# Cross-attention and experts in one kernel: key copies ahead of sums on ScalarE, sums dealt otherwise over the bodies, another order of steps among the experts

## What is computed

```python
def xattn(hs, at, mask):                       # 16 heads of 16
    q, k, v = proj(hs, Wq, bq), proj(at, Wk, bk), proj(at, Wv, bv)
    scores = clip(einsum('bhsd,bhtd->bhst', q, k) / 4, -50, 50)
    scores = clip(where(mask > 0.5, scores, -10000.0), -50, 50)
    probs = softmax(scores)
    probs = probs / (probs.sum(-1) + 1e-8)
    ctx = einsum('bhst,bhtd->bhsd', probs, v)
    delta = clip(rs, 0, 0.3) * nan_clean(ctx @ Wo.T + bo)
    return layernorm(delta) * ln_gamma + ln_beta

def ffn(hs):                                   # 8 experts, top 2 by softmax of hs @ router.T
    ...
    h = up * silu(gate)                        # each row in its two experts
    return sum over its two of (h @ down[e]) * score

x = x + tanh(g_xattn) * xattn(layernorm(x), ctx_2048, mask)
x = x + tanh(g_ffn) * ffn(layernorm(x))
```

## Time and profile before

| | |
|---|---|
| median of three runs | 290.21 us (290.14 to 292.1) |
| the profiled execution | 291.79 us, its span 290.1 us |
| TensorE busy | 236.3 us, 81% |
| VectorE busy | 179.2 us, 62% |
| ScalarE busy | 137.8 us, 48% |
| POOL busy | 62.5 us, 22% |
| chain that ended last | TensorE 56%, issue 19%, ScalarE 11%, VectorE 7%, POOL 5% |
| moved by DMA | 37.55 MB |

### The profile page before, as it was taken

The page is one execution under the profiler, slowest core; times in us unless marked ns, Lnnn a source line. Parts: engine busy times, 40 slices in busy tenths (PEclk is TensorE's granted clock), DMA queues, the critical chain, the costliest instruction groups (busy, mean ns, idle before and its releaser), DMA issues.

```text
span 290.1 us, 7184 instructions
## 1 busy us (share of the span) xinstructions
PE 236.3 (81%) x2704; PEld 181.2 (62%) x2704; DVE 179.2 (62%) x415; ACT 137.8 (48%) x220; POOL 62.5 (22%) x102
## 2 busy tenths in 40 slices
PE   0619389999999999859998629399899567999994
PEld 0309268888888888638886529296575336565653
DVE  7677805458899963365298923446379991494535
ACT  5135723567688678854378870220523406620110
POOL 2820021124245111101033200000625246210000
PEclk9999959999999999985999976859999997999998
DMA  7325801296798999988523000030000000020002
GB/s 177 90 54 162 353 5 39 67 329 239 274 292 325 341 385 427 398 260 316 214 83 137 2 0 2 3 64 5 0 0 0 0 0 2 0 63 1 2 0 64
DMA packets 12871, 37.55 MB, mean 129 GB/s; under 512 B 2321, under 2 KB 10017, under 8 KB 10529
## 3 DMA queue, kind: packets, MB, share of 16 engines
q1 hardware_dynamic: 12016, 36.65, 36.8%
q10 hardware_dynamic: 720, 0.40, 0.6%
q0 software_dynamic: 96, 0.00, 0.0%
HBM read 35.14 MB, written 0.92 MB: 124 GB/s over the span
## 4 chain that ended last, share of the span: by engine, by line
PE 56%; issue 19%; ACT 11%; DVE 7%; POOL 5%; DVEq 1%; POOLq 0%; ACTq 0%
PE bank L484 11%; PE bank L491 9%; PE bank L689 8%; PE bank L501 8%; PE bank L512 6%; PE bank L706 5%; ACT ctx_all L802 5%; ACT p L790 4%; POOL x_sb L461 4%; PE bank L476 3%; PE bank L593 1%; PE bank L469 1%; ACT normed L806 1%; PE bank L583 1%; DVE p L1171 1%
## 5 line engine op out<-in xcount | busy, mean ns | idle before, releaser
L790 ACT ACTIVATE p<-bank,mask_bias,mask_scale 125x896 f32<-125x896 f32 x38 | 39.6, 1093 | 43.8 <-PE bank L501 43.8
L484 PE MATMUL bank<-ctx_pair,wk 128*128 128x250 f32 x152 | 40.4, 410 | 5.9 <-issue 5.9
L689 PE MATMUL bank<-rowsT,gate_up 128*128 128x448 f32 x112 | 44.6, 541 | 0.0
L388 POOL COPY q_slot<-qbd 128x224 f32 x38 | 17.1, 453 | 95.2 <-PE bank L501 67.0
L491 PE MATMUL bank<-wv,ctx_pair 128*125 128x256 f32 x152 | 36.9, 387 | 0.0
L1002 DVE TENSOR_SCALAR p<-p 125x912 f32<-125x912 f32 x38 | 28.1, 754 | 14.1 <-ACT p L790 14.1
L484 PEld LDWEIGHTS bank<-ctx_pair,wk 128*128 128x128 f32 x152 | 29.1, 202 | 12.1 <-issue 7.0
L706 PE MATMUL bank<-down,act 128*112 128x256 f32 x128 | 31.8, 393 | 4.5 <-DVE act L1260 3.6
L802 ACT ACTIVATE ctx_all<-ctx_all 128x1500 f32<-128x1500 f32 x24 | 35.1, 1467 | 0.0
L491 PEld LDWEIGHTS bank<-wv,ctx_pair 128*125 128x125 f32 x152 | 29.3, 193 | 4.6
L706 PEld LDWEIGHTS bank<-down,act 128*112 128x112 f32 x128 | 23.1, 184 | 13.8 <-DVE act L1260 4.7
(11 more groups left out here) (147 smaller groups left out, 295.2 us busy)
## 6 DMA issues: line engine op xcount, KB each, us to landing
ctx_all<-ctx_dram SPq DMA_DIRECT2D x16, 1500.0 KB, 6.8
ctx_pair<-ctx_dram SPq DMA_DIRECT2D x38, 125.0 KB, 5.0
gate_up<-gate_up_dram SPq DMA_DIRECT2D x1, 2048.0 KB, 10.0
down<-down_dram SPq DMA_DIRECT2D x1, 1024.0 KB, 11.9
num<-acc SPq DMA_DIRECT2D x16, 57.0 KB, 2.7
x_sb<-x_dram SPq DMA_DIRECT2D x2, 448.0 KB, 6.4
out_dram<-x_sb SPq DMA_DIRECT2D x4, 224.0 KB, 2.4
wq<-wq_dram ACTq DMA_DIRECT2D x1, 256.0 KB, 4.4
```

Source lines behind the costliest of these rows:

```text
L388: nc.gpsimd.tensor_copy(targets[t], source).then_inc(flow.q_in, 1)
L484: mm = nc.tensor.matmul(bank[:, K_BANK, 2 * TT * m:2 * TT * (m + 1)], wk[:, k, P * m:P * (m + 1)], tile[:, :, k, :], start=(k == 0), stop= ...
L689: mm = nc.tensor.matmul(bank[:, GU_BANK[s % 2] + g, 0:HR], gate_up[:, e, k, g, :], rowsT[:, k, HR * h:HR * (h + 1)], start=(k == 0), stop= ...
L790: nc.scalar.activation(p_tile[:, t].rearrange("t (j n) s -> t j n s", j=4)[:, :, :, 0:S], bank[0:TT, 0:4, DEN * t:DEN * (t + 1)].rearrange ...
```

## The change

ScalarE's key copy of body i + 1 now stands behind the exponentials of body i, ahead of the sums. The sums follow two tables: `SUM_BODY[b]` is the body of batch b's first half, `LATER_BODY[b]` that of its second half where ScalarE does it; VectorE now does the second half of ten batches (`SHARE`), ScalarE of six. Bodies 20 and 21 have no sums. SyncE's `fetch_all(b)` stands at i = `SUM_BODY[b]` + 1, before the weights and before `pack(0)`. `add_delta(0, 1)` moves into body 21, `masked_sums(1)` behind pair 21, and among the experts the steps of TensorE, ScalarE, VectorE and POOL stand in another order; `delta_of` is parted in two.

```diff
--- before.py
+++ after.py
@@ -194,6 +194,10 @@
                 "spread1", "spread1b", "out1_0", "out1_1", "hT1_0", "hT1_1", "route1"]
         USE = {name: n for n, name in enumerate(USES)}
 
+        SUM_BODY = [6, 7, 8, 9, 10, 11, 12, 12, 13, 14, 14, 15, 16, 17, 18, 19]
+        LATER_BODY = [6, 7, 8, 9, 10, 11, 12, 13, 14, 15, 15, 16, 17, 18, 19, 19]
+        SHARE = 10
+
         def p_of(h):
             return (h % 8) // 2 * 4 + h // 8 * 2 + h % 2
 
@@ -210,7 +214,10 @@
 
             if b >= 0:
                 engine.wait_ge(sum_first, b + 1)
-                engine.wait_ge(sum_second[b // HB], b % HB + 1)
+                if b < SHARE:
+                    engine.wait_ge(sum_second[0], b + 1)
+                else:
+                    engine.wait_ge(sum_second[1], b - SHARE + 1)
 
         def misc(lo, hi, rows=P):
             return bank[0:rows, MISC_BANK, lo:hi]
@@ -304,15 +311,14 @@
                 sp.dma_start(tile[:], source.partition_broadcast(R2)).then_inc(late_in, 16)
             for i in range(10, NTAIL):
                 fetch_pair(i)
+                for b in range(B):
+                    if b >= STREAMS and SUM_BODY[b] + 1 == i:
+                        fetch_all(b)
                 if i == 16:
                     for tile, source in ((router, router_d), (gate_up, gate_up_d), (down, down_d)):
                         sp.dma_start(tile[:], source).then_inc(experts_in, 16)
                 if i == 19:
                     pack(0)
-                if i - 7 < B:
-                    fetch_all(i - 7)
-            for b in range(NTAIL - 7, B):
-                fetch_all(b)
             pack(1)
             out_rows = out_d.rearrange("(r p) h -> p r h", p=R2)
             for h in range(2):
@@ -445,13 +451,13 @@
             h_guess(1)
 
             for u in range(2 * NE):
-                if u == 4:
+                if u == 6:
                     delta_guess(2)
-                if u == 6:
+                if u == 7:
                     h_guess(2)
-                if u == 8:
+                if u == 10:
                     delta_guess(3)
-                if u == 10:
+                if u == 12:
                     h_guess(3)
                 pool.wait_ge(d_scaled, u + 1)
                 if u < 2:
@@ -707,7 +713,6 @@
                                               act[:, s % 2, R2 * t:R2 * (t + 1)], down[:, e, :], start=True, stop=True)
                     mm.then_inc(d_mm, 1)
 
-            masked_sums(1)
             pair_pv(NTAIL - 2)
             pe.wait_ge(experts_in, 48)
             pe.wait_ge(misc_out, USE["hT0_0"] + 1)
@@ -715,34 +720,37 @@
             expert_half(0, 0)
             expert_half(1, 0)
             pair_pv(NTAIL - 1)
+            masked_sums(1)
             h_transposes(0, 1)
             route(0)
             expert_half(0, 1).then_inc(gu_mm, 1)
             expert_half(1, 1).then_inc(gu_mm, 1)
             pe.wait_ge(main.acc_out, 2 * NTAIL)
             expert_out(0)
+            expert_in(2)
             use("spread1")
             spread_inverse(1, 0, misc(0, 2 * DEN)).then_inc(misc_mm, 1)
-            expert_in(2)
+            expert_out(1)
             use("spread1b")
             spread_inverse(1, 1, misc(0, 2 * DEN)).then_inc(misc_mm, 1)
-            expert_out(1)
             expert_in(3)
             project_out(1, 0)
             expert_out(2)
+            expert_in(4)
             project_out(1, 1)
-            expert_in(4)
             expert_out(3)
             expert_in(5)
             expert_out(4)
+            h_transposes(1, 0)
             expert_in(6)
-            h_transposes(1, 0)
             expert_out(5)
             expert_in(7)
+            expert_out(6)
             h_transposes(1, 1)
-            expert_out(6)
+            expert_out(7)
             route(1)
-            for s in range(NE - 1, 2 * NE):
+            expert_in(8)
+            for s in range(NE, 2 * NE):
                 if s + 1 < 2 * NE:
                     expert_in(s + 1)
                 expert_out(s)
@@ -801,6 +809,13 @@
                 mine = ctx_all[b % STREAMS][:, :, k, :]
                 nc.scalar.activation(mine, mine, ACT.Identity, accum_out=total[:, k, b:b + 1]).then_inc(
                     sum_first if k == 0 else sum_second[1], 1)
+
+            def sums_of(i):
+                for b in range(B):
+                    if SUM_BODY[b] == i:
+                        sum_all(b, 0)
+                    if b >= SHARE and LATER_BODY[b] == i:
+                        sum_all(b, 1)
 
             def normalise_rows(t, done):
                 nc.scalar.activation(normed[:, t], x_sb[:, t], ACT.Identity, bias=offset[:, t:t + 1],
@@ -867,13 +882,14 @@
             act_e.wait_ge(counted, 1)
             tiles = count_of(act_e)
             early_exps(NOPT - 1)
+            k_copy(main, k_sb, NOPT + 1)
             for i in range(NOPT, NTAIL):
-                pair_exps(i)
+                exps(main, p[i % 2], slots_of(i), i + 1)
                 if i == 21:
                     misc_rows(0, 0)
-                sum_all(i - NOPT, 0)
-                if i >= FIRST_B:
-                    sum_all(i - NOPT, 1)
+                if i + 1 < NTAIL:
+                    k_copy(main, k_sb, i + 2)
+                sums_of(i)
                 if i == 20:
                     h_rows(0)
             h_rows(1)
@@ -902,16 +918,19 @@
             gate_silu(1)
             for s in range(NE):
                 scale_expert(s)
-                gate_silu(s + 2)
+                if s == 4:
+                    misc_rows(1, 0)
+                if s == 6:
+                    misc_rows(1, 1)
+                if s == 7:
+                    exps_of_logits(1)
+                    gate_silu(NE)
+                if s != 6:
+                    gate_silu(s + 2)
                 if s == 3:
                     h_rows(2)
-                if s == 4:
-                    misc_rows(1, 0)
+                if s == 5:
                     h_rows(3)
-                if s == 5:
-                    misc_rows(1, 1)
-                if s == 6:
-                    exps_of_logits(1)
             for s in range(NE + 2, 2 * NE):
                 gate_silu(s)
 
@@ -1078,6 +1097,10 @@
                 nc.vector.tensor_tensor(flat, flat, bank[:, V_BANK, 0:2 * DEN], ALU.mult).then_inc(wide_out, 1)
 
             def delta_of(h, n):
+                delta_parts(h, n)
+                delta_whole()
+
+            def delta_parts(h, n):
 
                 dve.wait_ge(misc_mm, USE[f"out{h}_{n}"] + 1)
                 raw = fix_raw[:].rearrange("p n h -> p (n h)")
@@ -1090,7 +1113,12 @@
                 nc.vector.tensor_scalar(fix_neg[0:R2], raw, 0.0, lim[:, 1:2], ALU.min, ALU.max).then_inc(chain, 1)
                 nc.vector.tensor_scalar(finite[0:R2], raw, 0.0, 0.0, ALU.mult, ALU.is_equal).then_inc(chain, 1)
                 count[0] += 3
-                dve.wait_ge(chain, count[0] - 1)
+
+            def delta_whole():
+
+                raw = fix_raw[:].rearrange("p n h -> p (n h)")
+                out = delta[:].rearrange("p n h -> p (n h)")
+                dve.wait_ge(chain, count[0])
                 step(nc.vector.tensor_tensor(out, out, fix_neg[0:R2], ALU.add))
                 nc.vector.tensor_copy(spare[:, 0:1], spare[:, 1:2])
                 step(nc.vector.copy_predicated(out, finite[0:R2], raw))
@@ -1247,9 +1275,12 @@
                 elif i == 20:
                     delta_of(0, 1)
                     clips(main, p[i % 2], 2 * i + 1)
+                elif i == 21:
+                    add_delta(0, 1)
+                    clips(main, p[i % 2], 2 * i + 1)
                 else:
                     clips(main, p[i % 2], 2 * i + 1)
-                if i < FIRST_B:
+                if i - NOPT < SHARE:
                     sum_all(i - NOPT)
                 if i == 15:
                     masked_sums(0)
@@ -1271,31 +1302,32 @@
                                                    ALU.add).then_inc(d_out, 1)
 
             pair_sums(NTAIL - 2)
-            add_delta(0, 1)
+            h_offsets(0, 1)
             pair_sums(NTAIL - 1)
             masked_sums(1)
-            h_offsets(0, 1)
             shift_logits(0)
+            expert_ranks(0)
+            expert_weights(0)
+            gate(0)
             inverses(1)
-            gate(0)
+            gate(1)
             totals(1)
             misc_mix(0, "spread1")
-            gate(1)
-            expert_ranks(0)
-            expert_weights(0)
+            gate(2)
             misc_mix(1, "spread1b")
-            gate(2)
-            delta_of(1, 0)
             gate(3)
+            delta_parts(1, 0)
+            delta_whole()
+            gate(4)
             add_delta(1, 0)
-            gate(4)
+            delta_parts(1, 1)
             h_offsets(1, 0)
-            delta_of(1, 1)
             gate(5)
+            delta_whole()
+            gate(6)
             add_delta(1, 1)
-            gate(6)
+            gate(7)
             h_offsets(1, 1)
```

(1 more changed line is left out.)

## The result

The changed kernel takes 298.92 us (median; 297.24 to 302.22, four runs), the kernel before, on the same chip, 290.17. The ratio is 1.028, 95% interval 1.018 to 1.038: slower, where 285.8 us and faster was forecast. Some executions of any of these kernels come out some per cent longer at a lower granted clock; the ratios leave these out, the medians do not. The profiled execution took 297.24 us with a span of 295.6; the span before was 290.1, so the traces differ by 5.5 us and the medians by 8.7. I compare the traces.

The account below looks back on a forecast made before the run. TensorE bounds plain attention bodies, ScalarE's order bodies 15, 16 and 20, then SyncE's queue, and VectorE's row steps after attention. 13.9 - 1.8 - 8.8 - 7.7 = -4.4 us gave 285.8 us from 290.21; range 277.5 to 291.5.

Parts of the forecast that it names:

- Body 17: Attention: weights and pair 17 late in SyncE's queue, `pack(0)` behind `fetch_all(14)`, half clock after the stop; costs 13.9 us.
- the 1.9 that I had won ahead of it: Bodies 15 and 16: waits for `k_sb` go, so body 16's scores end at 119.8 instead of 121.7, -1.9 us.
- Rival 1: SyncE's queue: pair 17 is in time, `pack(0)` still waits for batch 11, +6.4 instead of +13.9; 278.3 us, chance 0.13.
- Bodies 18 to 21: Late attention: body 20's wait for keys goes, the wait for `h_rows(0)` shrinks; -1.8 us, bounds 0 to -3.5.
- End of attention: Scores 21 to first `expert_out`: sums done early, VectorE is the path; -8.8 us, bounds -9.9 and -6.0.
- the 1.1: End of attention: 1.1 us added for a clock that may be low, putting the first `expert_out` at 200.3.
- rival 3: End of attention: low clock, TensorE loses 2.8 us at half clock, 5.3 with first experts; 288.6 to 291.1, chance 0.18.
- Experts, first half: First `expert_out` to `expert_in(8)`: moved expert steps fill places where rows were awaited; -7.7 us, bounds -4 to -9.5.
- The walk: Experts' steps timed from first `expert_out`: TensorE waits 1.0 and 1.7 us for rows, `route(1)` ends at 42.8.
- the rule: Experts: VectorE and GpSimd's port pair is locked for a whole instruction; chains overlapping adds pay again, stage gains 4 only.
- The sign that I had named: Experts: waits for rows above 3 us would make the prediction wrong.
- each rival: Pair 17 in time 0.13; slow queue (291.3 us) 0.11; low clock 0.18; `pack(0)` not late (271.9 us) 0.08.

Follow-up runs that it names:

- Kernel 2: The changed kernel with SyncE's loop as before the change, all else kept; 279.83 us, ratio 0.964, and 279.81 us, ratio 0.969, when run again.
- kernel 3: The kernel before with the attention part of the change alone, end of attention and experts as before; 296.19 us, ratio 1.024.
- experiment 5: The changed kernel with the weights issued behind `pack(0)`: 291.35 to 299.22 us, no ratio; then with `pack(0)` also ahead of `fetch_all(14)`: 289.12 us, ratio 1.011.
- kernel 4: The kernel before with its attention loop (but `add_delta(0, 1)` in body 21) and the new order of everything behind it; 280.70 us, ratio 0.968.
- Kernel 7: The changed kernel with SyncE's old list and GpSimd's adds of expert rows cut to one column of 256; 269.59 us, ratio 0.937.
- kernel 8: The changed kernel with SyncE's old list and `add_delta(1, 1)` ahead of `gate(6)`; 276.63 us, ratio 0.958, and 274.79 us, ratio 0.955, when run again.
- both edits: The changed kernel with `pack(0)` ahead of `fetch_all(14)` and the experts' weights behind both, in body 19 of SyncE's list; 289.12 us, ratio 1.011.
- Kernels 2 and 9: The second is the changed kernel with SyncE's old list and the experts' old order; 281.18 us, ratio 0.987, and 279.92 us, ratio 0.972, when run again.

## Why the prediction was wrong

- **Body 17: mechanism right, size 2.3 short.** The weights at 113, the pair over 10 us in the queue, `pack(0)` behind `fetch_all(14)`, the half clock after the stop (3.58) came as forecast. Two terms missed: body 16's keys waited 1.87 for their own pair, which I had put at no wait (it used up the 1.9 that I had won ahead of it, itself 0.2 more than the waits of 0.5 and 1.2 add up to); and pair 17 landed at 128.7 instead of 126.0. Batch 10, from whose landing I counted, took 8.6 us from its issue at 106.67, so landed at 115.3 and not at 112.9; from there to the pair it was 13.4, as the 13.1 of the earlier trace rows said. Both misses are behind the one late batch; why it took 8.6 and not the 7.0 of the earlier trace rows was not tried. Kernel 2 shows that SyncE's list is the loss, kernel 3 that it needs none of the later edits; the table of experiment 5 splits it.
- **Rival 1 (pair 17 in time)** was priced at +6.4. Made true by the late weights, it measured 139.32 - 128.69 = +10.6. `pack(0)` went out no earlier than 126.48, and `den` was read 10.2 us after its first issue where I took 6.8, with whole batches issued at 122.19 and 126.09 ahead of it.
- **Bodies 18 to 21:** 2.8 against 1.8, inside the bounds.
- **End of attention:** 8.8 forecast, 6.6 seen, 9.4 in kernel 4. The chain was right, some of its terms were not. Clips 20 on VectorE end at 183.36, 1.2 behind scores 21 where I had them 0.8 ahead: 2.0. In kernel 4 they end 1.1 ahead of scores 21, which is most of the 2.8 between the two kernels. TensorE's last transposes and their copy took 1 us more than walked. `route(0)` at half clock took 3.15 instead of 1.7, 1.4 more, about what the 1.1 had been allowed for; from its end to `expert_out` it was 6.0, as walked without the allowance. The steps of VectorE between were 1.1 quicker. The clock, rival 3's mechanism, is there over the stretch, but it took 3.16 for the route in kernel 4 too and so does not part the two. First the clips 20 of the change, then kernel 4's route, then the change's stretch to the first `expert_out` (columns as in rows 8):

```profile
182.19 1.17 DVE L1021 TENSOR_SCALAR p<-p 125x912 f32<-125x912 f32 x2
```

```profile
176.52 3.16 PE L607 MATMUL bank<-router,rowsT 128*112 128x8 f32 x16 [0.62 <-ACT rowsT L835]
```

```profile
196.00:203.80 7.80, 7.80 (x27) 7.22 (x28) 5.11 (x19) 2.06 (x3) 0.00 (x0) 0.50 0.36 63
```

- **Experts, first half: the step that failed.** I forecast -7.7 from a walk with waits for rows of 1.0 and 1.7; they were 4.26 and 3.42, and the stage gave 1.3. The walk let VectorE's stretches under GpSimd's adds vanish because the guesses moved, and took `delta_of` at the 4.8 and `add_delta` at the 3.7 of the earlier trace rows, where no add ran. The stretches came back at the same total. I had written the rule that says so beside the sum, with a gain of 4, and did not use it. The walk also had `add_delta(1, 1)` behind gate 6 as if the gate were free; it stood 3.84 for an expert that the first delay had itself made late. The two waits are 5.0 us above the walk, and `expert_in(6)` behind the first, at 4.43 instead of 3.17, is 1.3 more: 6.3 of the 6.4 missing. Kernel 7 (no stretches, and the waits of the walk: 8 to 9 us faster than kernel 2) and kernel 8 (no gate ahead: 4) show both. The sign that I had named, waits for rows above 3 us, was there.
- **The sum:** of the 9.9 us between the forecast span (285.7) and the measured, the experts are 6.4, body 17 2.3, the end 2.2, less 1.0 from bodies 18 to 21. That alone puts the span at the change's 295.6, above every bound I gave: each rival carried one miss, and none carried body 17's, the end's and the experts' together. The medians lie 3.2 further apart than the spans, as told with the result.

## What to carry to other kernels

Where a queue is worked in order, check each moved request for what now stands ahead of it: two moves that look harmless (weights behind a later sum, a small pack behind a large prefetch) cost 11.5 us together at the spread, and the new list as a whole turned 3.6% faster into 2.8% slower. Where GpSimd works beside a VectorE chain, sum the stretches over all instructions of the chain before and after; an edit that frees the short ones may only hand them to the long ones. Put a step that is ready ahead of a gate that waits for an engine which itself waits for this chain.

## What the runs showed that I had not expected

- The clock's share is not tied to the waits one sees: the same section of the kernel, behind a wait of 3.42 us in both, ran 9.3 us in the changed kernel and 15.3 with `pack(0)` first, and 6 us of real gain vanished from the time. It took 15.3 and 15.2 with the weights late and with both edits, 10.5 with SyncE's old list. One kernel can differ in this way from itself: of the four executions with the weights late, one had a mean granted clock of 0.929 and a span of 289.6, the others 0.904 or 0.905 and 294.7 to 297.5. What decides was not found.
- Two stops that follow one another in attention (pair 17 and `den`) gave back almost exactly the sum of their separate gains (11.67 against 11.49), though the stops themselves do not stay as they were: the one ahead of the spread was 5.63 with `pack(0)` first, 10.88 in the change and 14.01 with pair 17 in time. The one for pair 17 hardly moved with `pack(0)` first (7.10 against 7.05).
- Runs on two chips don't settle a question of 1 or 2%. The medians of the kernel before were 291.05 us on one chip and 285.94 on another, though its executions there overlap (286.10 to 292.19, 284.79 to 291.39). Kernels 2 and 9, equal on one chip, had shown ratios of 0.964 and 0.987 from two.
